# Pairwise feature products: half-tile loops on TensorE and ScalarE, staged features, tiles laid in falling order, a first chunk of 66 pairs

## The reference

```python
NUM_FEAT = 40
_I, _J = np.triu_indices(NUM_FEAT, k=1)
proj = jnp.einsum('bnd,ed->bne', x, W)
out = proj[:, PAIR_I, :] * proj[:, PAIR_J, :]     # (512, 780, 128) fp32
```

## Time and profile before

| | before |
|---|---|
| median of 3 runs | 504.05 us (504.04 to 504.08) |
| time of the profiled execution | 504.14 us |
| its span | 502.4 us |
| DVE busy | 430.4 us (86%) |
| PE busy | 63.1 us (13%) |
| ACT busy | 54.1 us (11%) |
| q1 (SP's transfers), share of the 16 DMA engines | 99.3% |
| moved | 215.12 MB, 428 GB/s over the span |

### The profile page before, as it was taken

The page is one execution under the profiler, slowest core; times in us unless marked ns, Lnnn a source line. Parts: engine busy times, 40 slices in busy tenths (PEclk is TensorE's granted clock), DMA queues, the critical chain, the costliest instruction groups (busy, mean ns, idle before and its releaser), DMA issues.

```text
span 502.4 us, 1460 instructions
## 1 busy us (share of the span) xinstructions
PE 63.1 (13%) x481; PEld 57.3 (11%) x481; DVE 430.4 (86%) x184; ACT 54.1 (11%) x162; POOL 0.7 (0%) x6
## 2 busy tenths in 40 slices
PE   1999990000000000000000000000000000000000
PEld 1988890000000000000000000000000000000000
DVE  0899999999999998999899998899899999889100
ACT  1788880000000000000000000000000000000000
POOL 0000000000000000000000000000000000000000
PEclk9999996555555555555555555555555555555555
DMA  8999999999999999999999999999999999999998
GB/s 354 432 425 437 413 450 408 455 410 455 411 441 436 447 411 447 440 411 447 415 438 447 435 435 412 443 439 443 404 430 472 425 438 425 425 411 438 439 431 352
DMA packets 5623, 215.12 MB, mean 428 GB/s; under 512 B 624, under 2 KB 752, under 8 KB 752
## 3 DMA queue, kind: packets, MB, share of 16 engines
q1 hardware_dynamic: 5472, 214.96, 99.3%
q10 hardware_dynamic: 144, 0.07, 0.0%
HBM read 10.55 MB, written 204.47 MB: 428 GB/s over the span
## 4 chain that ended last, share of the span: by engine, by line
DVE 49%; DMA 41%; DVEq 1%; PE 1%; issue 0%; ACT 0%
DVE rows L234 49%; DMA out_dram<-rows 39%; DMA w_in<-in_L_rec_W_dram 2%; DVEq L84 1%; PE proj_ps L166 1%; PE turned_ps L156 0%; PE w_ps L175 0%; ACT rows L209 0%
## 5 line engine op out<-in xcount | busy, mean ns | idle before, releaser
L234 DVE TENSOR_TENSOR rows<-rows 128x896 f32<-128x896 f32 (+32 forms) x184 | 430.4, 2413 | 36.0 <-DMA out_dram<-rows 21.1
L166 PE MATMUL proj_ps<-w_turned,x_turned 128*128 128x128 f32 x320 | 54.8, 296 | 0.8 <-ACT x_turned L203 0.7
L166 PEld LDWEIGHTS proj_ps<-w_turned,x_turned 128*128 128x128 f32 x320 | 43.5, 197 | 5.4 <-ACT x_turned L203 1.9
L156 PE MATMUL turned_ps<-identity,rows 128*128 128x128 f32 x160 | 31.5, 283 | 1.4 <-ACT rows L209 1.4
L209 ACT COPY rows<-proj_ps 128x256 f32<-128x256 f32 x80 | 29.8, 372 | 10.2 <-PE proj_ps L166 4.9
L203 ACT COPY x_turned<-turned_ps 128x256 f32<-128x256 f32 x80 | 29.9, 378 | 2.2 <-PE turned_ps L156 2.0
L156 PEld LDWEIGHTS turned_ps<-identity,rows 128*128 128x128 f32 x160 | 20.8, 147 | 2.3 <-ACT rows L209 2.0
L175 PE MATMUL w_ps<-identity,w_in 128*128 128x128 f32 x1 | 0.4, 446 | 10.5 <-DMA w_in<-in_L_rec_W_dram 10.5
L199 ACT ACT_TABLE_LOAD x1 | 1.3, 1283 | 1.2 <-PEq L249 1.2
L175 PEld LDWEIGHTS w_ps<-identity,w_in 128*128 128x128 f32 x1 | 0.2, 181 | 10.5 <-issue 10.5
L199 ACT COPY w_turned<-w_ps 128x128 f32<-128x128 f32 x1 | 0.3, 265 | 8.6 <-PE w_ps L175 8.6
## 6 DMA issues: line engine op xcount, KB each, us to landing
out_dram<-rows SPq DMA_DIRECT2D x10, 4992.0 KB, 20.3
out_dram<-rows SPq DMA_DIRECT2D x8, 5568.0 KB, 27.5
out_dram<-rows SPq DMA_DIRECT2D x7, 6272.0 KB, 30.6
out_dram<-rows SPq DMA_DIRECT2D x6, 7168.0 KB, 33.8
rows<-in_r_x_dram SPq DMA_DIRECT2D x4, 2560.0 KB, 18.0
out_dram<-rows SPq DMA_DIRECT2D x1, 6912.0 KB, 35.6
out_dram<-rows SPq DMA_DIRECT2D x1, 6016.0 KB, 31.0
out_dram<-rows SPq DMA_DIRECT2D x1, 5376.0 KB, 27.5
```

Source lines behind the costliest of these rows:

```text
L156: last = pe.transpose(turned_ps[group % 2][:, n - a, :], feats(tile, n, n + 1)[:, 0, :], identity[:, :])
L166: last = pe.matmul(proj_ps[group % 2][:, k, :], x_turned[group % 2][:, k, :], w_turned[:, :], start=True, stop=True)
L234: last = dve.tensor_tensor(rows[:, slot_rows(tile, k, place, count), :], feats(tile, i, i + 1).broadcast_to([P, count, DIM]), feats(tile, ...
```

## The change

TensorE and ACT no longer have 80 groups written out. Each has a loop over half tiles of 20 features, 10 groups each: TensorE one loop of 8 turns, ACT one of 2 turns (the first tile, which has a load of its own to wait for) and one of 6. TensorE's instructions in the loop read fixed places: ACT first copies the two features of a group from `rows` to `staged0` or `staged1` (`stage`), and `turn` reads these. ACT's copies from and to `rows` take their place from the loop's register, and the waits of both engines compare semaphores with values computed from it. So that these places are a falling line through all halves, the tiles lie in falling order at the low end of `rows`, and the slots above and over them. `proj_ready` starts at 2. The chunks of the first tile are 66, eight times 80, and 74 pairs in place of ten times 78; the other tiles keep their sizes, and the number of chunks stays 34.

```diff
-CHUNK = [78, 87, 98, 112]
-FIRST_ROW = [[14, 170, 92], [201, 114, 27], [230, 132, 34], [20, 256, 144]]
+SIZES = [[66] + 8 * [80] + [74], 8 * [87] + [84], 7 * [98] + [94], 6 * [112] + [108]]
+FIRST_ROW = [[320, 160, 240], [120, 207, 294], [80, 178, 276], [276, 40, 152]]
...
         def feats(tile, a, b):
-            return rows[:, ROOM + tile * FEATURES + a:ROOM + tile * FEATURES + b, :]
+            first = (tiles - 1 - tile) * FEATURES
+            return rows[:, first + a:first + b, :]
+        staged = [sbuf(f"staged{k}", [P, GROUP, DIM]) for k in range(2)]
...
         def _(pe):
+            def turn(half, r):
+                pe.wait_ge(group_staged, half * HALF_GROUPS + (r + 1))
+                for n in range(GROUP):
+                    last = pe.transpose(turned_ps[r % 2][:, n, :], staged[r % 2][:, n, :], identity[:, :])
                 last.then_inc(group_turned, 1)
+            def project(half, r):
+                pe.wait_ge(x_turned_ready, half * HALF_GROUPS + (r + 1))
+                pe.wait_ge(proj_ready, half * HALF_GROUPS + (r + 1))
+                for n in range(GROUP):
+                    last = pe.matmul(proj_ps[r % 2][:, n, :], x_turned[r % 2][:, n, :], w_turned[:, :],
                                      start=True, stop=True)
                 last.then_inc(group_projected, 1)
...
             pe.wait_ge(w_ready, 1)
-            for group in range(1, GROUPS):
-                turn(0, group)
-                project(0, group - 1)
...
+            with pe.Fori(0, 2 * tiles) as half:
+                turn(half, 0)
+                for r in range(1, HALF_GROUPS):
+                    turn(half, r)
+                    project(half, r - 1)
+                project(half, HALF_GROUPS - 1)
...
+            def group_rows(half, r):
+                return bass.ds(half * -HALF + (2 * tiles * HALF - (r + 1) * GROUP), GROUP)
+            def stage(half, r):
+                act.copy(staged[r % 2][:, :, :], rows[:, group_rows(half, r), :]).then_inc(group_staged, 1)
...
+            def carry_projected(half, r):
+                act.wait_ge(w_in_ps, 1)
+                act.wait_ge(group_projected, half * HALF_GROUPS + (r + 1))
+                act.copy(rows[:, group_rows(half, r), :], proj_ps[r % 2][:, 0:GROUP, :]).then_inc(proj_ready, 1)
+            def half_tile(half):
+                stage(half, 0)
+                stage(half, 1)
+                for r in range(HALF_GROUPS):
+                    carry_turned(half, r)
+                    if r + 2 < HALF_GROUPS:
+                        stage(half, r + 2)
+                    if r > 0:
+                        carry_projected(half, r - 1)
+                carry_projected(half, HALF_GROUPS - 1)
+            act.wait_ge(first_loaded, 16)
+            with act.Fori(0, 2) as half:
+                half_tile(half)
+            act.wait_ge(tiles_loaded, 16 * (tiles - 1))
+            with act.Fori(2, 2 * tiles) as half:
+                half_tile(half)
```

More of the change, by code:

```diff
@@ L42 @@
 assert slots_overlap_only_old_chunks()
-assert GROUPS * GROUP == FEATURES and GROUPS % 2 == 0 and GROUP <= BANK_FEATURES
-def group_range(group):
-    return FEATURES - (group + 1) * GROUP, FEATURES - group * GROUP
+assert 2 * HALF_GROUPS * GROUP == FEATURES and HALF_GROUPS % 2 == 0 and GROUP <= BANK_FEATURES
 def group_of(i):
@@ L54, in chunk_range @@
 def chunk_range(tile, k):
-    return max(0, PAIRS - (k + 1) * CHUNK[tile]), PAIRS - k * CHUNK[tile]
+    return PAIRS - sum(SIZES[tile][:k + 1]), PAIRS - sum(SIZES[tile][:k])
 def chunk_number(tile, k):
@@ L81, in pairwise_products @@
     tiles = x.shape[0] // P
-    assert x.shape[0] == tiles * P and tiles == len(CHUNK)
+    assert x.shape[0] == tiles * P and tiles == len(SIZES)
     with ExitStack() as ctx:
@@ L116, in pairwise_products @@
         w_ready = sem("w_ready")
+        group_staged = sem("group_staged")
         group_turned = sem("group_turned")
@@ L152, in _ @@
         def _(pe):
[L153 to L157, removed]
-                last.then_inc(group_turned, 1)
[L160 to L166, removed]
+            def turn(half, r):
+                pe.wait_ge(group_staged, half * HALF_GROUPS + (r + 1))
+                for n in range(GROUP):
+                    last = pe.transpose(turned_ps[r % 2][:, n, :], staged[r % 2][:, n, :], identity[:, :])
+                last.then_inc(group_turned, 1)
+            def project(half, r):
[3 more added lines that the diff above has]
+                    last = pe.matmul(proj_ps[r % 2][:, n, :], x_turned[r % 2][:, n, :], w_turned[:, :],
                                      start=True, stop=True)
                 last.then_inc(group_projected, 1)
-            def last_banks_left(before):
-                pe.wait_ge(proj_ready, before + GROUPS)
             pe.wait_ge(identity_made, 1)
@@ L175, in _ @@
             pe.transpose(w_ps[:, :], w_in[:, :], identity[:, :]).then_inc(w_in_ps, 1)
-            pe.wait_ge(first_loaded, 16)
-            turn(0, 0)
             pe.wait_ge(w_ready, 1)
-            for group in range(1, GROUPS):
-                turn(0, group)
-                project(0, group - 1)
[L183 to L193, removed]
+            with pe.Fori(0, 2 * tiles) as half:
[4 more added lines that the diff above has]
+                project(half, HALF_GROUPS - 1)
         @block.scalar
@@ L197, in _ @@
             act.dma_start(w_in[:, :], w).then_inc(w_loaded, 16)
+            act.sem_inc(proj_ready, 2)
             act.wait_ge(w_in_ps, 1)
             act.copy(w_turned[:, :], w_ps[:, :]).then_inc(w_ready, 1)
[L201 to L216, removed]
+            def group_rows(half, r):
+                return bass.ds(half * -HALF + (2 * tiles * HALF - (r + 1) * GROUP), GROUP)
+            def stage(half, r):
+                act.copy(staged[r % 2][:, :, :], rows[:, group_rows(half, r), :]).then_inc(group_staged, 1)
@@ new lines, in carry_turned @@
+            def carry_turned(half, r):
+                act.wait_ge(group_turned, half * HALF_GROUPS + (r + 1))
+                act.copy(x_turned[r % 2][:, :, :], turned_ps[r % 2][:, 0:GROUP, :]).then_inc(x_turned_ready, 1)
+            def carry_projected(half, r):
+                act.wait_ge(w_in_ps, 1)
+                act.wait_ge(group_projected, half * HALF_GROUPS + (r + 1))
+                act.copy(rows[:, group_rows(half, r), :], proj_ps[r % 2][:, 0:GROUP, :]).then_inc(proj_ready, 1)
@@ L232, in _ @@
                             seen = group_of(i) + 1
-                            dve.wait_ge(proj_ready, tile * GROUPS + seen)
+                            dve.wait_ge(proj_ready, 2 + tile * GROUPS + seen)
                         last = dve.tensor_tensor(
```

15 lines of the change are left out of this document (9 added, 6 removed).

## The result

The changed kernel takes 504.92 us (median of 22 runs, 504.66 to 505.33), the old one beside it 504.05 (22 runs, 503.78 to 504.41). The ratio is 1.0017, with a 95% interval of 1.0011 to 1.0024: 0.87 us slower, clear of noise, and within the 0.2% that was called no change. The forecast was 504.7, or 0.65 slower. The profiled executions took 504.70 and 504.14 us.

What follows compares the result with a forecast made beforehand. DMA transfers (99.3% of the engines' time) bound the kernel, so only idle DMA time counts. The second store beginning 0.62 us later, added to 504.14, gives 504.76, and 504.7 for the median; range 503.7 to 505.8.

Steps and rivals of the forecast that it cites:

- first chunk of 66: First store: an unchanged ACT would give its issue at 24.73, closing the idle seam after the loads, worth up to 0.5 us.
- d = 1.20: Delay of DVE's start in us: 0.94 for staging plus 0.26 for register instructions, putting the second store's issue at 37.01.
- term of 0.94 for staging: Start of the chain: ACT's staging copies ahead of the first transposes make `carry_turned` begin 0.94 us later, at 12.36.
- 0.26 for register instructions: ACT before DVE's first product: register instructions and waits cost between nothing and 1.6 us; 0.26 was taken.
- The pace: First groups: ACT's three copies, 0.81 us, hide in TensorE's 1.28 us a group; taken as nothing, upper bound 0.96 us.
- later halves: First tile's second half begins at about 26.6 us, with 13 us of cover left for the loop's jump.
- The sum: Second store's packets begin at 37.81 against 37.19, so +0.62 us, giving 504.76 and, for the median, 504.7.
- The rest of the span the same, shifted by 0.6: After the second store: a sign expected in the profile, the span otherwise unchanged and 0.6 us later.
- Instruction transfers: TensorE's q8 transfers early in the span: their loss gains between nothing and 1.1 us; nothing was taken.
- rival of fetches at each jump: Loops' jumps back: TensorE fetches code seven times, 7.6 us if all fall on one DMA engine, 510.6; chance 0.04.
- Register instructions are dear: ACT's sequencer doesn't run ahead of a waiting copy, or the pace falls: 505.7 more likely, 507.0 at most; chance 0.20.
- theory B: Experiments' theory, as put for f1: each TensorE or ACT instruction makes one DMA engine later by some 2.5 ns.

Runs made afterwards that it cites:

- e4: Old kernel, with TensorE repeating 1,800 transposes of W in a loop after its last group, output the same: 512.52 us.
- h2: Old kernel, with GpSimd carrying out 4,400 instructions (waits already met, in a loop) beside TensorE's and ACT's work from 11 us on: 514.46 us.
- h1: Old kernel, with ACT carrying out 440 instructions (20 turns of waits already met) after its last copy: 504.90 us, ratio 1.0018.
- f2: Old kernel, with ACT carrying out 4,400 instructions (200 turns of waits already met) after its last copy: 513.95 us.
- f3: Old kernel, with TensorE carrying out 220 products of 512 columns in a loop after its last group: 505.96 us.
- e1: Changed kernel with the first tile back in ten chunks of 78 pairs: 506.27 us, ratio 1.0041.
- f1: Changed kernel with the first tile written out and read by TensorE without staging, loops with staging for the other three tiles only: 504.74 us, ratio 1.0014.
- e2: Old kernel with the new chunk sizes (first tile 66, eight of 80, 74): 503.77 us, ratio 0.9996.

## Why the prediction was right, and where it was not

The time, the sign and the class came out. Step by step:

- *The bound* was right: 99.3% stays, and the effects found are effects on DMA engines.
- *The first chunk of 66* closes the first seam: right. The idle time moves to the second store: right, seen in the windows.
- *d = 1.20* was too large. The term of 0.94 for staging was nearly right: DVE starts 0.78 later, with W landing 0.24 earlier (TensorE's first instruction at 10.27 in place of 10.51), so that relative to that the delay is 1.02. The earlier landing is chance: with the old start unchanged that instruction waited until 10.2 in e4 and 11.1 in h2. The 0.26 for register instructions was 0.08: they are done while W is being copied. The second store was issued at 36.48, not 37.01, 11.08 after the first, as worked out.
- *The pace* was right: TensorE's 1.28 us a group hides the third copy, and DVE waits no more than before. The later halves were faster than forecast: the second began at 22.35 in place of 26.6, and took ACT 9.8 us in place of 16 to 19, which only adds cover.
- *The sum.* With the measured issue the working of the prediction gives 37.28 for the second store's packets against 37.19, +0.1 in place of +0.62. The forecast of 504.7 stood near the result because that term was too large by 0.5 and another was missing. That is luck: the mechanism that the sum priced gave about 0.1 of the 0.87.
- *"The rest of the span the same, shifted by 0.6"* is the step that failed. For 14 of the 16 engines the shift is nil, and the one that ends last is 0.5 us later. The prediction had named this as a sign of being wrong: last packets further apart than before. What stands in its place is a cost of 2.1 to 2.4 ns of one DMA engine's time for each instruction that the program carries out. 442 instructions more at 2.2 ns make 0.97 us, by the runs with several thousand; measured are 0.87 for the change, and 0.90 for 440 idle instructions. This is shown by h1, e4, f2 and h2, by their times and their packets; that busy time does not matter is shown by f3 against e4.
- *Instruction transfers* at nothing: no run speaks against it. No q8 transfer is left, but what their loss is worth was not measured by itself. The rival of fetches at each jump is refuted for these loops: q14 has three transfers before and after. The Trainium skill (Runtime: NRT & Kernel Launch, "Instruction fetch mechanics") names a fetch for a taken branch only where its target lies outside the two pages held. The trace agrees, with no q8 transfer in seven jumps back.
- *The rivals.* "Register instructions are dear" had the right suspect and the wrong mechanism. They are cheap on their own engine and cost by their number: some 360 of the 442 are register instructions, branches and separate waits, the rest are the copies.

What stays open: by which way an instruction slows a DMA engine. Every run here is recorded by the profiler, also those that are only timed (each has its span), so the records themselves may be the traffic. The Trainium skill (NOTIFIC — Programmer's Manual, "The life of a record") says that each record of the notification block is written to a ring in memory over AXI. No run here shows whether these writes share that engine's path, or whether the cost remains without a profiler. Open are also the 0.3 to 0.8 us too much in e1, and the 0.4 by which f1's 504.74 lies above the 504.3 that theory B expected of it.

## What to carry to other kernels

In a kernel whose 16 DMA engines are never idle, the time is that of the last engine and not of the mean: look at the windows in which the last packets begin, and ask which engine is alone there. An instruction that no one waits for was not free here: some 2.2 ns each, waits already met as much as matmuls, so that a loop which shortens the program but adds instructions to carry out was slower. (Register instructions and branches were not run alone; they are 400 of f2's 4,400.) And closing an idle seam need not pay: e2 closed one of 0.5 us and gained 0.2 at the medians.

## What the runs showed of the hardware

- 4,401 instructions more on ACT or on GpSimd made the kernel 9.9 and 10.5 us longer, at unchanged transfers; after 500 us little but one DMA engine of 16 had packets left (share 0.06 and 0.08, 25 and 33 GB/s).
- One DMA engine's packets of 44,544 bytes took 1.69 to 1.72 us in the mean in place of 1.65 while such instructions ran, 2.2 to 2.3 ns more for each instruction, whether on TensorE, ACT or GpSimd (e4, f2, h2).
- ACT's first staged copy began 0.20 us after the copy before it began, though a branch, a register move and an ISA instruction stand between.
- A loop of TensorE with 60 matmuls, jumped back seven times, made no transfer of instructions in the span, where the written-out program made four.
- A store's first packet began some 0.8 us after its issue, where DMA engines stood idle for it, in both kernels (26.40 to 27.2, 36.48 to 37.3).
